# Mixture-of-experts outputs added into x in HBM by the scatter itself, with a table that says which blocks wait for the scatters ahead

## The reference

```
x = x + gat0(layernorm(x), adj)      # one-head graph attention with a mask
x = x + ffn0(layernorm(x))           # 8 experts, top 2 of them per token, hidden width 256
x = x + gat1(layernorm(x), adj)      # eight-head graph attention with the same mask
x = x + ffn1(layernorm(x))           # 8 experts, top 2, hidden width 512
# an expert layer, for each token and its two experts e0, e1:
y = w0 * (gelu(xn @ W1[e0] + b1[e0]) @ W2[e0] + b2[e0]) + w1 * (the same with e1)
```

## Time and profile before

| What | us |
|---|---|
| median of 3 runs (lowest to highest) | 2027.46 (2022.37 to 2035.77) |
| the profiled execution | 2038.51 |
| its span | 2036.8 |
| first to last scatter issued, layer 0 | 538.3 to 792.65 |
| first to last scatter issued, layer 1 | 1719.24 to 1987.60 |
| reading back and adding, layer 0 | 794.84 to 830.05 |
| reading back, adding, storing, layer 1 | 1989.79 to 2036.8 |

### The profile page before, as it was taken

How to read it: one execution, slowest core, us unless ns; L and a number is a source line. 1 busy time by engine, 2 the same in 40 slices (tenths; PEclk the granted TensorE clock), 3 DMA queues, 4 the chain that set the end, 5 groups by cost and what they waited for, 6 DMA issues and landing times. The chain is left out here.

```text
span 2036.8 us, 29795 instructions
## 1 busy us (share of the span) xinstructions
PE 1193.0 (59%) x10139; PEld 1024.5 (50%) x10139; DVE 1123.9 (55%) x2503; ACT 995.4 (49%) x1416; POOL 896.0 (44%) x725
## 2 busy tenths in 40 slices
PE   2767676641667762267675666777312206999970
PEld 2656666631556651155554555566212205999860
DVE  2765666552333333579898898999531222343323
ACT  3555555421444431188766866976312204666640
POOL 1011545476355564125325325432467662656550
PEclk8787877765777786578887887888555557999995
DMA  7532332112444443321212111210111125555518
GB/s 240 195 126 84 127 126 86 45 44 94 138 129 128 132 122 104 133 84 73 84 64 74 73 70 68 94 64 32 34 36 46 37 91 155 163 169 163 164 56 247
DMA packets 166117, 213.61 MB, mean 105 GB/s; under 512 B 29812, under 2 KB 121102, under 8 KB 164944
## 3 DMA queue, kind: packets, MB, share of 16 engines
q1 hardware_dynamic: 147792, 175.99, 27.7%
q0 software_dynamic: 18176, 35.72, 5.1%
HBM read 156.71 MB, written 58.56 MB: 106 GB/s over the span
## 5 line engine op out<-in xcount | busy, mean ns | idle before, releaser
L555 POOL DMA_INDIRECT y_dram<-f_ys,f_Xb x312 | 318.0, 1019 | 262.7 <-DVE f_ys L576 180.5
L1469 ACT ACTIVATE g_near<-g_s_row,g_steep 128x1024 fp8e4<-128x1024 f32 x352 | 369.3, 1134 | 2.3 <-issue 2.3
L1444 PE MATMUL g_bp<-g_G,g_near 128*128 128x102 bf16 x4096 | 247.6, 233 | 175.1 <-DVE g_near L1361 175.0
L1444 PEld LDWEIGHTS g_bp<-g_G,g_near 128*128 128x128 fp8e4 x4096 | 239.8, 113 | 203.3 <-issue 201.8
L204 POOL DMA_INDIRECT xs_dram<-r_row,r_pos x256 | 268.4, 1048 | 120.4 <-issue 80.2
L622 PE MATMUL f_ops<-f_w,f_g 128*128 128x128 f32 x1872 | 272.3, 290 | 42.1 <-ACT f_g L658 28.9
L622 PEld LDWEIGHTS f_ops<-f_w,f_g 128*128 128x128 f32 x1872 | 259.0, 204 | 68.8 <-ACT f_g L658 38.4
L658 ACT ACTIVATE f_g<-f_hps,f_ex 128x512 f32<-128x512 f32 x234 | 159.2, 689 | 199.4 <-PE f_hps L614 103.7
L1361 DVE TENSOR_TENSOR g_near<-g_near,g_mask 128x2048 uint32<-128x2048 uint32 x64 | 163.5, 2555 | 50.1 <-ACT g_near L1469 27.5
L1350 DVE TENSOR_SCALAR g_near<-g_s_row,g_nd 128x1024 fp8e4<-128x1024 f32 x160 | 158.3, 1038 | 0.0
L945 PE MATMUL attout<-V,Pt 128*128 128x129 f32 x1024 | 146.9, 304 | 9.5 <-DVE Pt L814 8.5
(11 more groups left out here) (223 smaller groups left out, 2164.1 us busy)
## 6 DMA issues: line engine op xcount, KB each, us to landing
raw<-in_adj SPq DMA_DIRECT2D x64, 512.0 KB, 6.5
g_s_row<-rows_dram SPq DMA_DIRECT2D x64, 512.0 KB, 3.6
f_Xb<-xs_dram SPq DMA_DIRECT2D x78, 288.0 KB
f_w<-in_L_ffn_W SPq DMA_DIRECT2D x78, 256.0 KB
f_yb<-y_dram SPq DMA_DIRECT2D x16, 1024.0 KB, 6.1
f_w<-in_L_ffn_W SPq DMA_DIRECT2D x78, 128.0 KB
mask_dram<-mask SPq DMA_DIRECT2D x16, 512.0 KB, 3.5
g_mask<-mask_dram SPq DMA_DIRECT2D x8, 1024.0 KB
```

What stands on the lines that cost most here:

```text
L555: pool.indirect_dma_start(y_d.rearrange("n k d -> (n k) d"), bass.IndirectOffsetOnAxis(ap=Xb[:, i % XB, r, D:D + 1].bitcast(U32), axis=0), ...
L1444: ins = pe.matmul(bp[h % 2][:, t // 4, (t % 4) * 6 * C:(t % 4 + 1) * 6 * C], near[:, h % 4, j, t * P:(t + 1) * P], G[:, s, j, h, :, :], st ...
L1469: ins = act.activation(near[:, h % 4, j, :], s_row[:, h % 4, :], ACT.Relu, scale=STEEP, bias=steep[:, s, j, h:h + 1], saturate=False)
```

## The change

The tensor `y_dram` and the last part of `phase_blocks` (read back, add, store) go. In their place x itself stands in HBM, in `x1_dram` for layer 0 and in the output tensor for layer 1, and GpSimd's scatters add their rows to it (`compute_op=ALU.add`). The destination number in a row of `xs_dram` is now the token's number, the same for both of its experts.

- `phase_gat0` stores each batch of x when its attention update is done (`store_x`, 8 stores of 512 KB, on SyncE ahead of a mask store). `phase_route` stores all of x, 4 MB, in one DMA behind its small loads.
- `phase_gat1` loads x back into SBUF: batch 0, batch 1, and the other six in one DMA, ahead of the mask. VectorE waits for the first two before its statistics, and for the third before its second step.
- Two blocks of different experts can now add to the same token. So block 1, 2 and 3 wait until the scatters of the block ahead have landed. A block from 4 on waits for those of block i - 2, and then reads a third row of `tab` into a register: 64 if the block is the first of its expert, else 0. It is added to the count that GpSimd waits for, so only the first block of an expert waits for the landing of block i - 1.
- `tab` gets that third row by two more small instructions of VectorE in `dve_table`, with a wait after each.

```diff
         pool.iota(blki[:, :], pattern=[[1, NB]], base=0, channel_multiplier=0).then_inc(s_c, 1)
-        pool.iota(idi[:, :, :], pattern=[[1, 2], [2 * P, NT]], base=0, channel_multiplier=2).then_inc(s_c, 1)
+        pool.iota(idi[:, :, :], pattern=[[0, 2], [P, NT]], base=0, channel_multiplier=1).then_inc(s_c, 1)
         pool.memset(pwc[:, 0, :], -0.5).then_inc(s_c, 1)
...
         dve.tensor_tensor(row[:, q, 1, :, D + 1], wgt[:, 1, :], row[:, q, 0, :, D + 1], ALU.mult).then_inc(s_meta, 1)
-        dve.tensor_scalar(ids[:, :, :], ids[:, :, :], float(2 * N), None, ALU.add).then_inc(s_t, 1)
+        dve.tensor_scalar(ids[:, :, :], ids[:, :, :], float(N), None, ALU.add).then_inc(s_t, 1)
         dve.wait_ge(s_pf, c + 1)
...
         dve.tensor_copy(tab[:, 0, :], tb[:, 0, :]).then_inc(s_t, 1)
+        dve.tensor_tensor(G[:, 0, :, 0], tb[:, 1, :], blk[:, :], ALU.is_equal).then_inc(s_ff, 1)
+        dve.wait_ge(s_ff, 1)
+        dve.tensor_scalar(tab[:, 2, :], G[:, 0, :, 0], 64.0, None, ALU.mult).then_inc(s_ff, 1)
+        dve.wait_ge(s_ff, 2)
         dve.scalar_tensor_tensor(tb[:, 1, :], tb[:, 1, :], -1.0, blk[:, :], ALU.mult, ALU.add).then_inc(s_t, 1)
...
     R = router(nc, sb, sem, K, L, px, Wr, br, W1, b1, W2, b2, gamma, beta, 3)
+    s_xst = sem("r1_xst")
...
             R.sp_setup(sp)
+            sp.dma_start(K["acc"][1], K["x"][:, :, :]).then_inc(s_xst, 16)
             R.sp_params(sp)
             R.sp_pads(sp)
+            sp.wait_ge(s_xst, 16)
...
     AHEAD, SKEW, GS, XB, WB, YB, TR = 2, 2, 4, 8, 5, 3, 3
-    last = L == 1
-    x_sb, ident, tab = K["x"], K["ident"], K["tab"]
-    rows_d, y_d, ex_d = K["xs_dram"], K["y_dram"], K["ex_dram"][L]
+    ident, tab = K["ident"], K["tab"]
+    rows_d, acc_d, ex_d = K["xs_dram"], K["acc_rows"][L], K["ex_dram"][L]
     S = lambda n: sem(f"f{L}_{n}")
...
             for i in range(YB):
-                sp.wait_ge(s_ys[i], 64 * (NB // YB))
-            for b in range(B):
-                wait(sp, s_add, 2 * (b - 1))
-                sp.dma_start(yb[:, b % 2, :, :, :], y_d[b * N:(b + 1) * N, :, :].rearrange("(t p) k d -> p t k d", p=P)).then_inc(s_yl[b % 2], 16)
-                if last and b:
-                    sp.wait_ge(s_add, 2 * b)
-                    sp.dma_start(K["out"][:, (b - 1) * NT:b * NT, :], x_sb[:, (b - 1) * NT:b * NT, :]).then_inc(s_out, 16)
-            if last:
-                sp.wait_ge(s_add, 2 * B)
-                sp.dma_start(K["out"][:, (B - 1) * NT:B * NT, :], x_sb[:, (B - 1) * NT:B * NT, :]).then_inc(s_out, 16)
-                sp.wait_ge(s_out, 16 * B)
+                sp.wait_ge(s_ys[i], 64 * len(range(i, NB, YB)))
...
             for i in range(NB):
+                if 1 <= i <= YB:
+                    pool.wait_ge(s_ys[(i - 1) % YB], 64 * ((i - 1) // YB + 1))
+                if i > YB:
+                    pool.wait_ge(s_ys[(i - 2) % YB], 64 * ((i - 2) // YB + 1))
+                    other = pool.value_load(tab[0:1, 2, i:i + 1], min_val=0, max_val=64)
+                    pool.wait_ge(s_ys[(i - 1) % YB], other + 64 * ((i - 1) // YB))
+                    pool.nop(nofuse=True)
                 pool.wait_ge(s_ysc, i + 1)
                 for r in range(4):
-                    pool.indirect_dma_start(y_d.rearrange("n k d -> (n k) d"), bass.IndirectOffsetOnAxis(ap=Xb[:, i % XB, r, D:D + 1].bitcast(U32), axis=0),
-                                            ys[:, i % YB, r, :], None, bounds_check=2 * B * N - 1, oob_is_err=False).then_inc(s_ys[i % YB], 16)
+                    pool.indirect_dma_start(acc_d, bass.IndirectOffsetOnAxis(ap=Xb[:, i % XB, r, D:D + 1].bitcast(U32), axis=0),
+                                            ys[:, i % YB, r, :], None, bounds_check=B * N - 1, oob_is_err=False, compute_op=ALU.add).then_inc(s_ys[i % YB], 16)
...
             gate_block(NB - 1)
-
-            for b in range(B):
-                dve.wait_ge(s_yl[b % 2], 16 * (b // 2 + 1))
-                xb = x_sb[:, b * NT:(b + 1) * NT, :]
-                dve.tensor_tensor(xb, xb, yb[:, b % 2, :, 0, :], ALU.add).then_inc(s_add, 1)
-                dve.wait_ge(s_add, 2 * b + 1)
-                dve.tensor_tensor(xb, xb, yb[:, b % 2, :, 1, :], ALU.add).then_inc(s_add, 1)
...
+            def store_x(c):
+                sp.wait_ge(s_up, 2 * c + 2)
+                sp.dma_start(K["acc"][0][:, c * NT:(c + 1) * NT, :], x_sb[:, c * NT:(c + 1) * NT, :]).then_inc(s_xst, 16)
+
             def step(b):
...
                     R.sp_params(sp)
+                if b >= 2:
+                    store_x(b - 2)
                 for hf in range(2):
...
                 step(b)
+            for c in range(B - 3, B):
+                store_x(c)
             for hf in range(2):
...
             R.sp_pads(sp)
+            sp.wait_ge(s_xst, B * 16)
...
             sp.dma_start(ab[:, :], a.rearrange("(o e) -> o e", o=1).to_broadcast([P, 2 * HD])).then_inc(s_w, 16)
+            for c0, c1, s_in in ((0, 1, s_x0), (1, 2, s_x1), (2, B, s_x2)):
+                sp.dma_start(x_sb[:, c0 * NT:c1 * NT, :], K["acc"][0][:, c0 * NT:c1 * NT, :]).then_inc(s_in, 16)
...
                 if isinstance(b, int) and b == -1:
+                    dve.wait_ge(s_x0, 16)
+                    dve.wait_ge(s_x1, 16)
                     normalise_at(0, STATS)
                     normalise_at(0, NORM)
+                if isinstance(b, int) and b == 0:
+                    dve.wait_ge(s_x2, 16)
                 for h in range(NH):
...
         K["xs_dram"] = nc.dram_tensor("xs_dram", (ROWS, RW), FP32, kind="Internal").ap()
-        K["y_dram"] = nc.dram_tensor("y_dram", (B * N, 2, D), FP32, kind="Internal").ap()
+        x1_dram = nc.dram_tensor("x1_dram", (B * N, D), FP32, kind="Internal").ap()
+        K["acc_rows"] = [x1_dram, out.rearrange("b n d -> (b n) d")]
+        K["acc"] = [v.rearrange("(t p) d -> p t d", p=P) for v in K["acc_rows"]]
         K["ex_dram"] = [nc.dram_tensor(f"ex{L}_dram", (E, P, H // P + 2 + D), FP32, kind="Internal").ap() for L, H in ((0, 256), (1, 512))]
-        K["tab"] = keep("tab", [P, 2, NB], I32)
-        K["out"] = out.rearrange("b (t p) d -> p (b t) d", p=P)
+        K["tab"] = keep("tab", [P, 3, NB], I32)
         K["rmax"] = bass.bass_isa.ReduceOp.max```

GpSimd's instructions at the start of the blocks of layer 0, before (each pair of rows is one block; its first scatter waits for `ys`, here under the name of an earlier phase's semaphore, since semaphores are used again):

```order
L550 UNCONDITIONAL_BRANCH [waits barrier_Pool_Activation_PE_DVE_SP_gather]
L555 DMA y_dram<-f_ys,f_Xb 16384x128 [waits r0_lgr]
L555 DMA y_dram<-f_ys,f_Xb 16384x128 x3
L555 DMA y_dram<-f_ys,f_Xb 16384x128 [waits r0_lgr]
L555 DMA y_dram<-f_ys,f_Xb 16384x128 x3
```

More of the change, by code:

```diff
@@ L139, in router @@
         pass
+    s_ff = S("ff")
     def sp_setup(sp):
@@ L504, in phase_blocks @@
     ys = T("ys", [P, YB, 4, D], FP32)
-    yb = T("yb", [P, 2, NT, 2, D], FP32)
     hps = [pb(f"f{L}_hps{i}", [P, TB], FP32) for i in range(4)]
@@ L515, in phase_blocks @@
     s_ys = [S(f"ys{i}") for i in range(YB)]
-    s_yl = [S(f"yl{i}") for i in range(2)]
-    s_add, s_out = S("add"), S("out")
     with nc.Block() as block:
@@ L729, in phase_gat0 @@
     s_neg, s_e, s_up = sem("g0_neg"), sem("g0_e"), sem("g0_up")
-    s_setup, s_wt, s_dv = sem("g0_setup"), sem("g0_wt"), sem("g0_dv")
+    s_setup, s_wt, s_dv, s_xst = sem("g0_setup"), sem("g0_wt"), sem("g0_dv"), sem("g0_xst")
     x_v = x_dram.rearrange("b (t p) d -> p (b t) d", p=P)
@@ L1170, in phase_gat1 @@
     s_prod, s_sum, s_rden, s_on, s_x = (S(n) for n in "prod sum rden on x".split())
+    s_x0, s_x1, s_x2 = (S(n) for n in "x0 x1 x2".split())
     E1, EVAC_E1 = 1, 5
```

## The result

| | median us | lowest to highest | runs |
|---|---|---|---|
| before | 2024.91 | 2018.99 to 2035.77 | 4 |
| after | 2078.49 | 2076.64 to 2080.67 | 4 |

The changed kernel takes 1.0259 times as long [1.0212, 1.0306]: slower by 2.1 to 3.1%. The forecast was 1970 us, in a range from 1950 to 2060, and is wrong, in sign too. Its rival A, an adding scatter that is slower to issue, is what happened.

The account below looks back on a forecast made before the run. It took layer 0 as paced by the five weight buffers' loop, layer 1 by TensorE, with DMA-bound tails. Terms -46.1 - 35.2 + 2.0 + 2 + 12 + 4 + 4.4 = -56.9 us from 2027.5 gave 1970 us, range 1950 to 2060.

Parts of the forecast that it names:

- rival A: Expert stages: adding scatter slower to issue, up to 1.47 us, GpSimd becomes the bound; 2093 us, chance 0.25.
- step 5: GpSimd's queue: a register load ahead of 35 of 39 blocks, 0.66 us each, 23 us a layer.
- step 7: Expert stages: of 54 us new GpSimd work a layer, most hides in 55 and 69 us of room; +12 and +4.
- Step 6: GpSimd's landing waits, 10 a layer: landing 4.4 us after a scatter's start, 3.1 us a time, 31 a layer.
- Steps 1 and 2: Tails behind the expert stages go: -46.1 us in layer 1, -35.2 us in layer 0.
- the landings: End of each layer: the last scatter's landing is 2.2 us longer, +4.4 us in all.
- Step 3: Start of gat1: x is loaded back, statistics begin about 7 us after its first DMA; +2.0 us.
- Step 4: Stores of x, 4 MB in gat0 and 4 MB in route: +2 us in all, bounds 0 and 18.
- the last sign of the forecast's failure: Layer 1: forecast wrong if TensorE's granted clock falls from 0.95 because it waits for buffers.
- The turning point: Expert stages: the change turns slower than before when one scatter takes more than about 1.24 us.
- Rival B: Expert stages: adding scatters land slowly, at 8.63 us, an expert's start costs 7.35 us; 2031 us, chance 0.12.

Follow-up runs that it names:

- the 64-row writes: Changed kernel with each block's four scatters made a write and an add of 128 rows, a write and an add of 64: 1966.16 us, output incomplete.
- the constants: Changed kernel with the register load replaced by constants saying which blocks wait: 2067.57 us, ratio to before 1.0546.
- the pause kernel: Changed kernel with scatters that write instead of adding, each followed by a GpSimd memset nobody reads: 2007.53 us, before on this chip 2038.99.

## Why the prediction was wrong

*The step that failed is the price of a scatter.* The sum has no term for it: steps 5 to 7 count 4 x 1.28 us a block from the earlier trace rows as if an adding scatter were issued like a writing one. It takes 1.543 us, so a block takes 4 x 1.845 = 7.38 us and not 5.12 (5.78 with step 5). That is over the pace of both stages, 6.55 and 6.91, so GpSimd sets the pace, and the room in which step 7 hid the waits is gone. With this put right, and what the runs showed for steps 5 and 6, the same method gives: layer 0, 39 x (7.38 - 6.55) = 32, plus 25 of waits and 10 of longer scatters, 67 (measured 66.2); layer 1, 39 x (7.38 - 6.91) = 18, plus 35, 53 (measured 53.8). The prediction had 12 + 4. The difference, 104 us, is more than the whole miss of 99.1 (42.2 against -56.9).

*The argument that misled*: the router's scatters take 1.05 us on average with other rows and another tensor, "so the engine's time hardly depends on what is moved". True, and the 64-row writes confirm it; but size is one property of the instruction and its kind another. No row of before held an adding scatter, and the nearest row was near in size only. The upper end that the prediction took, 1.468 us, was still 0.08 too low, and rival A's 2093 came close to 2078.5 because two other prices of it were too high: the register load (0.66, really 0) and the wait (3.1, really 2.3).

*A rule of the Trainium skill points the same way, though neither page has a price for an adding scatter.* "DMA: Bandwidth & Descriptors" (section "SWDGE vs HWDGE vs iDMA") says that for a DMA issued from GpSimd a core there computes descriptors, the orders that the DMA engines work off, in pairs: one reads and one writes. "Collectives: The Full Stack" (section "The bandwidth ceiling: the fold count and why AG ≠ RS ≠ AR") says that the reduce step of a collective emits two reading descriptors per chunk, for the local and for the arriving operand. Carried over to an adding scatter, which is a guess, that makes three descriptors of two, and as an estimate from these pages 1.46 us of 0.97. The measured 1.543 has the direction, and nearly the size at 128 rows. As a mechanism it is not borne out: by it 64 rows would add half as much as 128, and they add 0.47 against 0.52. The four prices, 0.95 and 1.03 plain, 1.42 and 1.55 adding, go by the instruction.

Point by point:

- *Steps 1 and 2, the tails*: right. -46.1 - 35.2 + 4.4 for the landings was forecast, -76.9; measured -74.4. The end of layer 0 and the start of gat1:

```profile
854.95 1.54 POOL L557 DMA_INDIRECT x_dram<-f_ys,f_Xb  x1 [0.30 <-issue]
861.49 0.34 SPq L1216 DMA_DIRECT2D g_Wext<-in_L_gnn_W  x1
...
862.36 2.93 SPq L1219 DMA_DIRECT2D x_sb<-x_dram  x3
865.33 10.92 SPq L1237 DMA_DIRECT2D g_mask<-mask_dram  x1
...
869.21 0.49 DVE L1299 BATCH_NORM_STATS2 g_stats<-x_sb 128x6 f32<-128x128 f32 x2 [2.78 <-DMA x_sb<-x_dram]
```

  6.5 us from the last scatter to gat1's first DMA (sign: under 7); in layer 1, 6.6 to the end of the span (sign: within 6, missed by 0.6, of which 0.57 is the longer scatter).
- *Step 3, the reload*: statistics 7.7 us after gat1's first DMA (sign: about 7). gat1 and route together +1.6 us.
- *Step 4, the stores*: +2 forecast; the stretch up to the first load of rows came out 4.05 shorter, so a cost isn't seen.
- *Step 5, the register load*: 0.66 us a block forecast, 0 measured; the constants changed nothing. Step 5 was priced from SyncE's queue, where nothing ran beside the loads; on GpSimd the 1.54 us of a scatter runs beside them.
- *Step 6, the waits*: 4.4 us from the last scatter's start forecast, 4.07 measured at block 3 and 4.35 at block 5; but the longer scatter is part of it. The wait adds 2.2 to the gap at block 3, and costs 2.3 over all (forecast 3.1).
- *Step 7, the cover*: forecast that 54 us of new work would find 55 and 69 of room. The new work was 39 x 2.26 = 88 us of scatters plus 35 in each layer, and the room differs by chip: on the one where before was profiled again it isn't there in layer 0. The ratio is 1.026 on one kind and 1.053 on the other.
- *Clock*: the last sign of the forecast's failure, TensorE's granted clock in layer 1 below 0.95, was seen too (0.90).
- *The turning point*: forecast 1.24 us a scatter. On the faster kind of chip, between 0.97 us (-48) and 1.54 us (+102), a straight line crosses zero at 1.15 us. On the other kind it crosses at about 1.45, between the pause kernel (1.675 - 0.30 = 1.375, -31.5) and after (+39.5, the first chip's 2078.5 against this one's before). Both are interpolations, and both join points of two chips.

Rival B (slow landing) is out: the gap at an expert's start is 2.2 to 3.1 us, not 7.

## What to carry to other kernels

An operation that no row of the trace holds is the first thing to price, before the sum: here a term of 88 us a layer hung on an instruction of another kind, and one block of four scatters of different kinds would have told. Before moving work onto an in-order queue, divide the stage by the queue's own issue time (4 x 1.28 of 6.55 us left 1.4 us a block; the change needed 2.3). An edit that saves a tail once is weighed against a price that is paid 156 times a layer, padding blocks included.

## What the runs showed of the hardware

- An adding indirect DMA on GpSimd holds the engine 1.54 us, a writing one 0.97 (128 rows of 512 B); 1.42 and 0.95 for 64 rows. The longest in each layer, 2.05, are first behind a wait.
- The adding form also loads the DMA engines more. In layer 0 the queue that carries GpSimd's scatters went from 4977 packets and a share of 9.5% to:

```profile
q0 software_dynamic: 22047, 8.30, 29.9%
```

  for the same 8.3 MB, here over 317 us (540 to 857) in place of 255. Three times the share is more than the doubling that the prediction assumed, and over the longer stretch it is 3.9 times the engines' time. No run shows that it cost time, with 0.54 of the DMA engines busy.
- A register load from SBUF on GpSimd costs nothing where a scatter runs ahead of it.
- The same kernel differs by chip about as much as by this change: before takes 2025 and 2039 us on two chips, 1961 and 1966 on two others. The changed kernel takes 2078 and 2069 on one of each kind: its stages, paced by GpSimd, are the same length on both, so what makes the first two slower hardly shows in them.
